# Two memsets of 128x1280 on GpSimd between one field's gathers and the next field's, in a float32 recommendation tower

## The chip, the cores and the metric

One core of a Trainium2 chip. The metric is the time of the whole program on the device in microseconds. Before the change two runs gave 289.72 and 292.36 us, median 291.04.

## The reference

512 samples have 39 fields each. A field's id picks a row of 32 numbers from its table (1000 to 125000 rows). Each pair of fields (i, j) is joined by a 32x32 weight, which gives one number for each of 741 pairs and each sample; these, with 16 dense numbers, go through a small MLP (757 to 512 to 256 to 1).

```python
e = jnp.stack([tbl_0[ids[:, 0]], ..., tbl_38[ids[:, 38]]], axis=1)      # 512 x 39 x 32
z = jnp.einsum('bpc,apc,bpa->bp', e[:, ROW, :], w, e[:, COL, :])        # 741 pairs
h = jnp.concatenate([z, dense_ctx], axis=1)
h = jnp.maximum(h @ W_top1 + b_top1, 0.0)
h = jnp.maximum(h @ W_top2 + b_top2, 0.0)
y = h @ W_top3
```

## The kernel before

The 39 fields are put in an order of 10 blocks of four (the last has three). Blocks 0, 1 and 3 hold twelve fields with tables of 1000 rows, the "hot" ones. Their rows are fetched by one-hot matmuls: SP loads the tables (`tab`) and the ids, ACT and DVE (`rest`, `split`) part each table in three bf16 pieces (`parts`), DVE compares ids with row numbers (L629, into `hot`), and PE multiplies (L688, step `look`): for each hot block eight parts `c`, each of 12 matmuls, which end with one semaphore step of `hot_used`. The last of these look-ups, that of block 3, goes to `z_ps`. Two of the six `rest` steps (L410) are on GpSimd (POOL).

The other seven blocks (2, 4, 5, 6, 7, 8, 9) are gathered. POOL issues for each field four indirect DMAs (L514), each for 128 samples, 27 fields and so 108 gathers in all, into `gathered`, which has three buffers: before block 6 POOL waits until block 2 has been transposed, before block 7 until block 4 has, before block 8 until block 5 has, before block 9 until block 6 has (`turned`). PE transposes a block (L700, step `keep`) when its rows are in; ACT copies it to `eT` (L567) and with DVE makes the split copies in `stack`.

The pairs are then done in 70 groups of tiles (step `tiles`): PE multiplies `stack` with weights from `wring` (L719, 210 matmuls), DVE multiplies the result with `eT` (L658), PE sums over the 32 numbers with `sel` (L735, step `sums`). The ring's chunks are copied by SP from `w_hi` and `w_lo`; the low parts of chunk columns 2 and 3 are made by POOL (L401). Chunk column 2 is first used by group 37, column 3 by group 56. Between the groups lie matmuls of the MLP's first layer (L750, step `early`), whose rounds POOL adds up at the end (L528).

One list, `PLAN`, sets the order of PE, ACT, DVE and SP. In it block 4's transpose stands ahead of group 5, block 5's ahead of group 13, block 6's ahead of group 22, block 7's ahead of group 31, block 8's ahead of group 42, block 9's ahead of group 54. POOL has its own order: gathers block by block, with the four steps of `POOL_WORK` behind the gathers of a field: a `rest` step of hot block 1 (needed for the look-up of block 1) behind block 2's last field, a `rest` step of the third hot block behind block 4's first field, `w_lo` columns 2 and 3 behind block 8's first and last field.

Of the kernel before, what the change touches and what calls it, by code (L numbers as in the profile page):

```python
# [43 lines left out]
P = 128  # L44
# [18 lines left out]
HP = HOT_ROWS // NSLICE  # L63
HOT_BUFS = 4
GATHER_BUFS = 3
STACKS = 3
HOT_FIELDS = [f for f in range(F) if TABLE_ROWS[f] == HOT_ROWS][:G * NHOT]

# [12 lines left out]
def in_block(J):  # L81
    return min(G, F - G * J)
# [140 lines left out]
def turns(J):  # L223

    return TURNS.index(J) + 1
# [48 lines left out]
def dlrm_tower(nc, tables, ids, hot_ids, dense_t, wst, w1, w2, columns, y):  # L274
    with ExitStack() as ctx:
        def sb(name, shape, dt=F32):
            return ctx.enter_context(nc.sbuf_tensor(name, shape, dt))

        def sem(name):
            return ctx.enter_context(nc.semaphore(name))  # L280
# [4 lines left out]
        sel = sb("sel", [P, ZM, K])  # L285
        gathered = sb("gathered", [P, GATHER_BUFS, NCHUNK, P])
        eT = sb("eT", [P, NBLK, B])
        hi_lo = sb("hi_lo", [P, 2, 2, B])
        stack = sb("stack", [P, STACKS, G, B])
        w_lo = sb("w_lo", [P, NWCOL, WCOLS])  # L290
# [7 lines left out]
        b2_sb = columns_sb[:, M1:M1 + M2]  # L298
        w3_sb = columns_sb[:, M1 + M2:]
        y_sb = sb("y_sb", [1, B])  # L300

        room = sb("room", [P, (NZ + M1) * B])
        z_sb = room[:, 0:NZ * B].rearrange("p (k b) -> p k b", k=NZ)
# [60 lines left out]
        stack_lo_made = sem("stack_lo_made")  # L364
        stacked = [sem(f"stacked{i}") for i in range(STACKS)]
        w_hi_made = sem("w_hi_made")
# [15 lines left out]
        y_made = sem("y_made")  # L382
        y_kept = sem("y_kept")
        y_out = sem("y_out")

        mlp_loads = [(w1_sb, w1.rearrange("(k p) n -> p k n", p=P)),
                     (w2_sb, w2.rearrange("(k p) n -> p k n", p=P)),
# [10 lines left out]
        def w_lower(engine, c):  # L398

            engine.wait_ge(w_hi_made, c + 1)  # L400
            engine.tensor_tensor(w_lo[:, c, :].bitcast(F32R), w_lo[:, c, :], w_hi[:, c, :],  # L401
                                 ALU.subtract).then_inc(w_lo_made[c], 1)

        def table_rest(engine, h, i):

            of = slice(G * h, G * h + G)
            engine.wait_ge(part_made, SPLITS.index((h, i)) + 1)
            if i == 1:
                engine.wait_ge(rest_made[h], 1)
            engine.tensor_tensor(parts[2][0:HP, of, :] if i else tab[0:HP, of, :], tab[0:HP, of, :],  # L410
                                 parts[i][0:HP, of, :], ALU.subtract).then_inc(rest_made[h], 1)

        def wait_z(engine, zb):

            engine.wait_ge(z_kept, zb + 1)
            if zb in DENSE_BLOCKS:
                engine.wait_ge(dense_in[zb], 16 * sum(first // P == zb for first, _ in DENSE_ROWS))
# [4 lines left out]
        def _(sp):  # L422
# [35 lines left out]
            for step in PLAN:  # L458
# [3 lines left out]
                if step[0] == "stack":  # L462
                    J = step[1]
                    sp.wait_ge(stack_hi_made, turns(J))
                    sp.wait_ge(stack_lo_made, turns(J))
                    slot = J % STACKS
                    sp.dma_start(stack[P // 2:P, slot, 0:in_block(J), :],
# [23 lines left out]
        @block.gpsimd  # L491
        def _(pool):
            pool.memset(ident[:, :], 0.0).then_inc(consts_zero, 1)
            pool.memset(sel[:, :, :], 1.0).then_inc(consts_zero, 1)
            pool.iota(slice_rows_int[:, :], pattern=[[1, NSLICE]], base=0,
                      channel_multiplier=NSLICE).then_inc(rows_numbered, 1)
            pool.wait_ge(consts_zero, 2)
            pool.affine_select(out=ident[:, :], in_=ident[:, :], compare_op=ALU.not_equal, fill=1.0, base=0,
                               pattern=[[-1, P]], channel_multiplier=1).then_inc(consts_made, 1)

            pool.affine_select(out=sel[:, :, :], in_=sel[:, :, :], compare_op=ALU.is_ge, fill=0.0, base=0,
                               pattern=[[P, ZM], [-K, K]], channel_multiplier=1).then_inc(consts_made, 1)
            pool.wait_ge(consts_made, 2)
            pool.affine_select(out=sel[:, :, :], in_=sel[:, :, :], compare_op=ALU.is_ge, fill=0.0, base=K - 1,
                               pattern=[[-P, ZM], [K, K]], channel_multiplier=-1).then_inc(consts_made, 1)
            pool.wait_ge(ids_in, 16)

            for n, J in enumerate(GATHERED):
                if n >= GATHER_BUFS:
                    pool.wait_ge(turned, n - GATHER_BUFS + 1)  # L510
                for r in range(in_block(J)):
                    f = ORDER[G * J + r]
                    for b in range(NCHUNK):
                        pool.indirect_dma_start(  # L514
                            gathered[:, n % GATHER_BUFS, b, K * r:K * r + K], None, tables[f],
                            bass.IndirectOffsetOnAxis(ap=ids_sb[:, F * b + f:F * b + f + 1], axis=0),
                        ).then_inc(rows_in[J], 16)
                    work = POOL_WORK.get((J, r))
                    if work is not None and work[0] == "rest":
                        table_rest(pool, *work[1:])  # L520
                    elif work is not None:
                        w_lower(pool, work[1])
            for n in range(1, len(ROUNDS)):
                for i, m in enumerate(LAST_FIRST):
                    pool.wait_ge(early_kept, M1 * n + m + 1)
                    if n > 1:
                        pool.wait_ge(early_added, M1 * (n - 2) + i + 1)
                    pool.tensor_tensor(early_sum[0][m], early_sum[0][m], early_sum[n][m],  # L528
                                       ALU.add).then_inc(early_added, 1)

        @block.scalar
        def _(act):
# [3 lines left out]
            for step in PLAN:  # L536
# [31 lines left out]
                elif step[0] == "halve":  # L568
# [4 lines left out]
                    if turns(J) > 2:  # L573
                        act.wait_ge(lo_made, turns(J) - 2)
                    act.activation(hi_lo[0:n, slot, 0, :].bitcast(F32R), eT[0:n, J, :],
                                   ACT.Copy).then_inc(hi_made, 1)
                    if J >= STACKS:
                        act.wait_ge(tiles_made, LAST_GROUP[J - STACKS] + 1)
                    for r in range(in_block(J)):
                        ins = act.activation(stack[0:K, J % STACKS, r, :].bitcast(F32R),  # L580
                                             eT[K * r:K * r + K, J, :], ACT.Copy)
# [32 lines left out]
        def _(dve):  # L614
            for step in PLAN:
                if step[0] == "w_lo":
                    w_lower(dve, step[1])
                elif step[0] == "rest":
                    table_rest(dve, *step[1:])
                elif step[0] == "look":  # L620
                    J, c0, c1 = step[1:]
# [47 lines left out]
        def _(pe):  # L669
# [8 lines left out]
            for step in PLAN:  # L678
# [14 lines left out]
                elif step[0] == "keep" and step[1] in GATHERED:  # L693
                    J = step[1]
                    n = K * in_block(J)
                    at = GATHERED.index(J) % GATHER_BUFS
                    pe.wait_ge(rows_in[J], 16 * in_block(J) * NCHUNK)
# [5 lines left out]
                elif step[0] == "tiles":  # L703
# [10 lines left out]
                    for i, tile in enumerate(tiles):  # L714
                        for k, (src, _) in enumerate(tile):
                            c = passes // WCHUNK
                            if passes % WCHUNK == 0:
                                pe.wait_ge(wring_in[c % WSLOTS], 16 * G * (c // WSLOTS + 1))
                            mm = pe.matmul(t_ps[g % 2][:, i, :],  # L719
                                           wring[:, c % WSLOTS, passes % WCHUNK, :].bitcast(F32R),  # L720
                                           stack[:, J % STACKS, src - G * J, :].bitcast(F32R),
                                           start=(k == 0), stop=(k == len(tile) - 1))
                            passes += 1
# [86 lines left out]
```

## Time and profile before

| | |
|---|---|
| runs, median (lowest to highest) | 291.04 us (289.72 to 292.36) |
| span of the profiled execution | 285.0 us |
| runs' median less that span | 6.0 us |
| PE busy | 198.8 us (70%), 974 matmuls |
| DVE busy | 146.6 us (51%) |
| POOL busy | 134.8 us (47%), of it 104.9 us in 108 gathers |
| ACT busy | 97.5 us (34%) |
| granted TensorE clock, mean | 0.844 |

The span runs from the first to the last instruction of the profiled execution. What the time of a run has beyond it lies before and after the program's instructions; this execution has no time of its own beside the span, so the difference is taken to the median of the two runs. The rows count microseconds from the span's start. The granted clock is 1.00 at 2.4 GHz and 0.50 at 1.2 GHz. "Idle before, releaser" names what ended an engine's wait; "issue" is a wait for nothing that the profile shows, and "remote" is a semaphore whose setter the profile can't name by the time of its record.

### The profile page before, as it was taken

The page shows a single profiled execution, that of the slowest core. Times are in us where ns is not written, and L with a number is a line of the kernel's source. Part 1 is how long each engine was busy: PE and PEld are TensorE (multiplying, and loading weights), DVE is VectorE, ACT ScalarE, POOL GpSimd, SP SyncE. Part 2 cuts the span into 40 slices and gives each one's busy share as a digit, 9 for nine tenths or more (in the row PEclk, how much of TensorE's full clock was granted, in tenths as well). Part 3 has the DMA queues.
Part 4 walks back from the last instruction along what each step waited for, and adds up shares of the span by engine and source line. Part 5 has one row for each costly group of instructions (what it writes and reads, how often), then busy time and mean ns, then how long its engine had stood idle before and what let it go on. Part 6 is the DMA issues. An engine that isn't in the chain of part 4 may idle for free.

```text
span 285.0 us, 2687 instructions
## 1 busy us (share of the span) xinstructions
PE 198.8 (70%) x974; PEld 73.5 (26%) x974; DVE 146.6 (51%) x115; ACT 97.5 (34%) x142; POOL 134.8 (47%) x134
## 2 busy tenths in 40 slices
PE   0048668453212277738798197699899999999996
PEld 0012223000000033213333032243333334344341
DVE  0353794101000027824794266389599779898230
ACT  2516899300000047830540071037127127110032
POOL 7774767777777300776587887200042015007000
PEclk9999797755555559795999669599999999999999
DMA  4869779700000003997266018148715846450000
GB/s 134 257 210 300 285 177 212 164 16 13 14 13 13 9 0 74 300 207 148 50 158 166 12 41 183 41 96 167 167 33 118 183 98 129 98 121 1 0 2 0
DMA packets 11352, 31.40 MB, mean 110 GB/s; under 512 B 3230, under 2 KB 7098, under 8 KB 10379
## 3 DMA queue, kind: packets, MB, share of 16 engines
q1 hardware_dynamic: 7882, 29.45, 42.1%
q0 software_dynamic: 3456, 1.78, 3.5%
q8 instruction: 8, 0.13, 0.2%
q14 instruction: 6, 0.04, 0.0%
HBM read 12.34 MB, written 0.00 MB: 43 GB/s over the span
## 4 chain that ended last, share of the span: by engine, by line
PE 51%; issue 18%; DMA 9%; DVE 7%; SPq 6%; another core or an unknown queue 4%; ACT 3%; DVEq 0%; ACTq 0%
PE t_ps L719 16%; PE z_ps L735 15%; PE z_ps L688 9%; DMA mlp<-tbl 6%; PE side_ps L750 5%; DMA wring<-w_lo 4%; DVE prod L658 3%; SPq L425 2%; PE t_ps L777 2%; DVE prod L629 2%; SPq L431 1%; SPq L475 1%; PE t_ps L765 1%; PE t_ps L770 1%
## 5 line engine op out<-in xcount | busy, mean ns | idle before, releaser
L658 DVE TENSOR_TENSOR prod<-t_ps,eT 128x1536 f32<-128x1536 f32 (+2 forms) x70 | 109.9, 1600 | 79.3 <-PE t_ps L719 49.7
L514 POOL DMA_INDIRECT gathered<-tbl,ids_sb x108 | 104.9, 971 | 53.5 <-issue 31.4
L719 PE MATMUL t_ps<-stack,wring 128*128 128x512 f32 x210 | 72.9, 464 | 12.2 <-issue 6.7
L735 PE MATMUL z_ps<-prod,sel 128*32 128x512 f32 x380 | 57.5, 645 | 4.6 <-issue 4.6
L719 PEld LDWEIGHTS t_ps<-stack,wring 128*128 128x128 f32 x210 | 38.3, 205 | 65.8 <-issue 39.5
L688 PE MATMUL z_ps<-prod,room 125*32 125x512 bf16 x72 | 21.0, 534 | 34.1 <-issue 33.3
L528 POOL TENSOR_TENSOR room<-room,w_hi 128x512 f32<-128x512 f32 x3 | 3.9, 1286 | 66.3 <-ACT w_hi L603 66.3
L629 DVE TENSOR_SCALAR prod<-mlp,slice_rows 125x2048 bf16<-125x2048 f16 x18 | 14.8, 856 | 23.0 <-remote 23.0
L587 ACT ACTIVATE stack<-hi_lo 32x512 fp32r<-32x512 f32 x39 | 24.6, 629 | 2.6 <-issue 1.2
L580 ACT ACTIVATE stack<-eT 32x512 fp32r<-32x512 f32 x39 | 24.4, 625 | 1.0 <-PE t_ps L719 0.7
L750 PE MATMUL side_ps<-room,mlp 128*128 128x512 f32 x32 | 18.4, 660 | 7.7 <-ACT eT L567 7.6
L688 PE MATMUL t_ps<-hot,room 125*32 125x512 bf16 x48 | 6.3, 560 | 18.6 <-DVE hot L629 17.6
L564 ACT ACTIVATE eT<-z_ps 128x512 f32<-128x512 f32 x1 | 0.6, 597 | 50.1 <-PE z_ps L688 50.1
L688 PEld LDWEIGHTS z_ps<-prod,room 125*32 125x32 bf16 x72 | 4.3, 115 | 50.2 <-issue 49.6
L688 PE MATMUL t_ps<-prod,room 125*32 125x512 bf16 x144 | 13.5, 524 | 5.3 <-DVE prod L629 4.8
L735 PEld LDWEIGHTS z_ps<-prod,sel 128*32 128x32 f32 x380 | 8.4, 111 | 30.7 <-issue 24.5
L567 ACT ACTIVATE eT<-side_ps 128x512 f32<-128x512 f32 (+1 forms) x7 | 4.2, 595 | 34.7 <-PE side_ps L700 22.4
L592 ACT ACTIVATE room<-z_ps 128x512 f32<-128x512 f32 x6 | 3.6, 598 | 26.2 <-PE z_ps L735 19.3
L603 ACT ACTIVATE w_lo<-side_ps 128x512 f32<-128x512 f32 x9 | 5.3, 592 | 20.0 <-PE side_ps L750 18.9
L410 DVE TENSOR_TENSOR mlp<-mlp,room 125x1024 f32<-125x1024 f32 x3 | 3.7, 1226 | 15.8 <-issue 13.0
L528 POOL TENSOR_TENSOR room<-room,w_lo 128x512 f32<-128x512 f32 x9 | 11.3, 1286 | 0.0
L554 ACT ACTIVATE room<-mlp 125x1024 bf16<-125x1024 f32 x6 | 6.3, 1054 | 13.7 <-DMA mlp<-tbl 12.4
(49 smaller groups left out, 113.5 us busy)
## 6 DMA issues: line engine op xcount, KB each, us to landing
wring<-w_hi SPq DMA_DIRECT2D x30, 224.0 KB
wring<-w_lo SPq DMA_DIRECT2D x30, 224.0 KB
stack<-stack SPq DMA_DIRECT2D x9, 512.0 KB
w_lo<-wst SPq DMA_DIRECT2D x4, 896.0 KB, 15.2
eT<-hot_ids SPq DMA_DIRECT2D x3, 1024.0 KB
gathered<-tbl,ids_sb POOLq DMA_INDIRECT x108
mlp<-w SPq DMA_DIRECT2D x1, 1536.0 KB
mlp<-tbl SPq DMA_DIRECT2D x12, 125.0 KB
```

Of the source, the lines that this page charges most:

```text
L425: sp.dma_start(tab[0:HP, n, :], tables[HOT_FIELDS[n]].rearrange("(p c) d -> p (c d)", c=NSLICE))\
L514: pool.indirect_dma_start(gathered[:, n % GATHER_BUFS, b, K * r:K * r + K], None, tables[f], bass.IndirectOffsetOnAxis(ap=ids_sb[:, F * b ...
L528: pool.tensor_tensor(early_sum[0][m], early_sum[0][m], early_sum[n][m], ALU.add).then_inc(early_added, 1)
L554: act.activation(parts[i][0:HP, of, :], tab[0:HP, of, :], ACT.Copy).then_inc(part_made, 1)
L580: ins = act.activation(stack[0:K, J % STACKS, r, :].bitcast(F32R), eT[K * r:K * r + K, J, :], ACT.Copy)
L587: ins = act.activation(stack[K:2 * K, J % STACKS, r, :].bitcast(F32R), hi_lo[K * r:K * r + K, turns(J) % 2, 1, :], ACT.Copy)
L629: dve.tensor_scalar(hot[n % HOT_BUFS][0:HP, :, :], ids_half[J % 2][0:HP, :, :], slice_rows[0:HP, c:c + 1], None, ALU.is_equal).then_inc(ho ...
L658: dve.tensor_tensor(prod[:, g % XSLOTS, 0:n, :], t_ps[g % 2][:, 0:n, :], field, ALU.mult).then_inc(multiplied, 1)
L688: mm = pe.matmul(look_ps[J][K * r:K * r + K, :], parts[i][0:HP, G * J + r, K * c:K * c + K], hot[n % HOT_BUFS][0:HP, r, :], start=(c == 0 ...
L719: mm = pe.matmul(t_ps[g % 2][:, i, :], wring[:, c % WSLOTS, passes % WCHUNK, :].bitcast(F32R), stack[:, J % STACKS, src - G * J, :].bitcas ...
L735: mm = pe.matmul(z_ps[K * (u % G):K * (u % G) + K, :], sel[:, u // G, :], prod[:, g % XSLOTS, t - TILE_BASE[g], :], start=(u < G), stop=(u ...
L750: mm = pe.matmul(side_ps[:, :], w, x, start=(i == 0), stop=last)
```

## The change

A new scratch tile `pause` of 128x1280 float32. Behind the four gathers of every field, and ahead of the `POOL_WORK` step that may follow them, POOL clears it twice. Each of these memsets waits on the semaphore `paused` until all earlier ones are complete. Nothing reads the tile.

```diff
+PAUSE = 1280
+PAUSES = 2
@@
+        pause = sb("pause", [P, PAUSE])
@@
+        paused = sem("paused")
+        pauses = []
@@
+        def rest_a_while(engine):
+
+            for _ in range(PAUSES):
+                if pauses:
+                    engine.wait_ge(paused, len(pauses))
+                engine.memset(pause[:, :], 0.0).then_inc(paused, 1)
+                pauses.append(None)
@@
                             bass.IndirectOffsetOnAxis(ap=ids_sb[:, F * b + f:F * b + f + 1], axis=0),
                         ).then_inc(rows_in[J], 16)
+                    rest_a_while(pool)
                     work = POOL_WORK.get((J, r))
```

On POOL, from the first gather on, the kernel before has this order (L514 gathers, 128x32 each; L410 the two `rest` steps):

```order
L514 DMA gathered<-tbl,ids_sb 128x32 x16
L410 TENSOR_TENSOR room<-mlp,room 125x1024
L514 DMA gathered<-tbl,ids_sb 128x32 x4
L410 TENSOR_TENSOR room<-mlp,room 125x1024
L514 DMA gathered<-tbl,ids_sb 128x32 x64
```

The changed kernel has at the same place:

```order
L527 DMA gathered<-tbl,ids_sb 128x32 x4
L423 MEMSET pause 128x1280 x2
L527 DMA gathered<-tbl,ids_sb 128x32 x4
L423 MEMSET pause 128x1280 x2
L415 TENSOR_TENSOR room<-mlp,room 125x1024
L527 DMA gathered<-tbl,ids_sb 128x32 x4
L423 MEMSET pause 128x1280 x2
L415 TENSOR_TENSOR room<-mlp,room 125x1024
L527 DMA gathered<-tbl,ids_sb 128x32 x4
L423 MEMSET pause 128x1280 x2
```

Two memsets now stand behind each four gathers, so that the first `rest` step has four pairs ahead of it and the second has five. The other place is block 8 and 9, the last gathers. Before:

```order
L401 TENSOR_TENSOR w_lo<-w_lo,w_hi 128x1792
L514 DMA gathered<-tbl,ids_sb 128x32 x12
L401 TENSOR_TENSOR w_lo<-w_lo,w_hi 128x1792
L514 DMA gathered<-tbl,ids_sb 128x32 x12
```

And changed, from the first of these `w_lo` steps on:

```order
L406 TENSOR_TENSOR w_lo<-w_lo,w_hi 128x1792
L527 DMA gathered<-tbl,ids_sb 128x32 x4
L423 MEMSET pause 128x1280 x2
L527 DMA gathered<-tbl,ids_sb 128x32 x4
L423 MEMSET pause 128x1280 x2
L527 DMA gathered<-tbl,ids_sb 128x32 x4
L423 MEMSET pause 128x1280 x2
L406 TENSOR_TENSOR w_lo<-w_lo,w_hi 128x1792
L527 DMA gathered<-tbl,ids_sb 128x32 x4
L423 MEMSET pause 128x1280 x2
```

Here too a pair follows every field, three of them between the two `w_lo` steps. The other engines' orders are as before.

## Rows read from the trace of the kernel before

**Rows 1.** The page: span, PE's busy tenths in 40 slices, a load's time to landing.

```profile
span 285.0 us, 2687 instructions
...
PE   0048668453212277738798197699899999999996
...
ids_sb<-ids SPq DMA_DIRECT2D x1, 78.0 KB, 1.9
```

**Rows 2.** Busy by stretch: PE, PEld, DVE, ACT, POOL; granted clock, DMA share, GB/s.

```profile
40.30:47.10 6.80, 5.79 (x76) 2.31 (x77) 5.11 (x8) 6.65 (x12) 5.24 (x6) 0.75 0.98 203
52.00:77.00 25.00, 10.98 (x24) 1.74 (x24) 1.59 (x2) 1.09 (x2) 18.92 (x20) 0.52 0.20 40
77.00:96.00 19.00, 4.10 (x7) 0.71 (x7) 0.00 (x0) 0.00 (x0) 14.37 (x16) 0.50 0.07 13
96.00:103.00 7.00, 2.83 (x5) 0.40 (x4) 0.00 (x0) 0.00 (x0) 0.00 (x0) 0.50 0.01 2
...
212.00:236.00 24.00, 23.71 (x118) 8.66 (x116) 20.49 (x14) 9.03 (x15) 5.67 (x5) 1.00 0.64 137
236.00:285.00 49.00, 46.75 (x200) 18.42 (x196) 30.02 (x23) 12.85 (x21) 7.88 (x7) 1.00 0.22 47
```

**Rows 3.** Timeline of the look-ups: start, duration, engine, line, idle before and releaser.

```profile
32.49 1.47 PE L688 MATMUL t_ps<-hot,room 125*32 125x512 bf16 x12 [2.69 <-DVE hot L629]
...
66.83 0.83 DVE L629 TENSOR_SCALAR prod<-mlp,slice_rows 125x2048 bf16<-125x2048 f16 x1 [10.48 <-remote]
...
80.12 0.59 PE L688 MATMUL z_ps<-prod,room 125*32 125x512 bf16 x1 [2.21 <-issue]
...
103.20 0.60 ACT L564 ACTIVATE eT<-z_ps 128x512 f32<-128x512 f32 x1 [50.10 <-PE z_ps L688]
```

**Rows 4.** Timeline, three more waits for results of PE.

```profile
25.60 2.08 DVE L629 TENSOR_SCALAR prod<-mlp,slice_rows 125x2048 bf16<-125x2048 f16 x3 [3.65 <-remote]
...
162.44 0.60 ACT L567 ACTIVATE eT<-side_ps 128x512 f32<-128x512 f32 x1 [12.35 <-remote]
...
179.89 0.60 ACT L592 ACTIVATE room<-z_ps 128x512 f32<-128x512 f32 x1 [6.89 <-remote]
```

**Rows 5.** Groups of POOL by line: count, busy us, mean ns, idle before.

```profile
L514 POOL DMA_INDIRECT gathered<-tbl,ids_sb x108 | 104.9, 971 | 53.5 <-issue 31.4 <-PE side_ps L700 21.7 <-DMA ids_sb<-ids 0.4
...
L410 POOL TENSOR_TENSOR room<-mlp,room 125x1024 bf16<-125x1024 f32 x2 | 4.9, 2434 | 6.5 <-ACT room L554 6.5
...
L504 POOL TENSOR_SCALAR_AFFINE_SELECT sel<-sel 128x256 f32<-128x256 f32 x1 | 0.4, 445 | 0.1
L494 POOL MEMSET sel<- 128x256 f32 x1 | 0.3, 312 | 0.0
...
L493 POOL MEMSET ident<- 128x128 f32 x1 | 0.2, 205 | 0.3 <-POOLq L802 0.3
```

**Rows 6.** Timeline of POOL, where bursts of gathers begin or have ended.

```profile
27.22 2.44 POOL L410 TENSOR_TENSOR room<-mlp,room 125x1024 bf16<-125x1024 f32 x1 [3.88 <-ACT room L554]
...
37.76 2.42 POOL L410 TENSOR_TENSOR room<-mlp,room 125x1024 bf16<-125x1024 f32 x1 [2.67 <-ACT room L554]
...
113.61 1.25 POOL L514 DMA_INDIRECT gathered<-tbl,ids_sb  x1 [17.68 <-PE side_ps L700]
...
137.76 0.94 POOL L514 DMA_INDIRECT gathered<-tbl,ids_sb  x1 [3.99 <-PE side_ps L700]
...
142.46 4.06 POOL L401 TENSOR_TENSOR w_lo<-w_lo,w_hi 128x1792 fp32r<-128x1792 f32 x1
...
161.38 3.98 POOL L401 TENSOR_TENSOR w_lo<-w_lo,w_hi 128x1792 fp32r<-128x1792 f32 x1
...
179.54 0.94 POOL L514 DMA_INDIRECT gathered<-tbl,ids_sb  x1 [0.30 <-issue]
```

**Rows 7.** Line 700, transposes of block 7 and of block 9: first and last start.

```profile
L700 PE MATMUL side_ps<-ident,gathered x4: 270/272/272, 188.4 to 188.7; 128*128 128x128 f32 x4
...
L700 PE MATMUL side_ps<-ident,gathered x4: 273/273/315, 236.0 to 236.3; 128*96 128x128 f32 x4
```

## The prediction

> **What bounds the kernel now.** I read the page first. TensorE (PE) shows tenths 3, 2, 1, 2, 2 in the five slices from 64 to 100 us, and 8 or 9 from 185 us to the end [rows 1]. So there are two kernels in one: a late part that TensorE bounds, and an early part in which nearly nothing runs. The table by stretch says the same: from 212 to 236 us PE is busy 23.7 of 24.0 us, from 236 to 285 us 46.8 of 49.0, both at full clock; but from 52 to 77 us it runs 24 matmuls, from 77 to 96 us 7, and DVE, ACT and the DMA engines stand idle too. Only GpSimd (POOL) works there, 14.4 of 19.0 us: it issues gathers [rows 2].
>
> Next I asked the timeline who waits. PE in that stretch is in the last one-hot look-up (L688, hot block 3, 96 matmuls). Each matmul's record is 0.6 us, but they start 2.8 us apart "by issue", while the same line ran 76 matmuls in 6.8 us from 40.3 us [rows 2, 3]. DVE waits 10.48 us and ACT 50.10 us for its results [rows 3]. Three more places have the same sign, a "remote" wait for a PE result whose matmuls had long been recorded: 3.65 us to 25.60, 12.35 us to 162.44, 6.89 us to 179.89 [rows 4].
>
> The last view is POOL's timeline. Gathers run in bursts: 3.0 to 23.3, 29.8 to 35.1, 40.3 to 95.9, 113.6 to 133.8, 137.8 to 142.4, 146.7 to 161.4, 165.5 to 180.5 (108 gathers; where POOL did or awaited something else stands in [rows 6], with the wait that tells when the burst before it ended). All four late releases stand inside or just behind a burst of 12 or more gathers: 25.60 is 2.3 us after one ended, 162.44 is 1.1 us after, 179.89 within the last gather. The long stretch ends at 103, 7.1 us after the last of 44 gathers in a row. After 180.5 us there are no gathers and no such wait. And the two bursts of only four gathers passed without harm. So my reading is that PE's work completes late while gathers are issued without a break, that the lag grows with the length of the burst (slow from some 5 us into it), and that it drains in 1 to 7 us after it. In the stretch from 45 to 103 us 7 of that look-up's 8 parts of 12 matmuls complete; at the rate of [rows 2], 6.8 us for 76 matmuls, these 84 take 7.5 us. Some 50 us are lost there.
>
> **The change, part by part.** Behind every fourth gather come two memsets of 128x1280, each waiting for the one before: 27 times, 54 memsets, also before the two `rest` and the two `w_lo` steps that POOL carries.
>
> One memset: the trace has none of that size. Two others give a line, 205 ns for 128 columns and 312 ns for 256 [rows 5]: 0.84 ns a column, so 0.31 + 1024 x 0.84 ns = 1.17 us. From below, the slope without a fixed part gives 1.07 us. From above, 312/256 = 1.22 ns a column gives 1.56 us; the two-input subtraction, 2434 ns for 1024 columns [rows 5], would give 3.0 us, but it reads two tensors and this reads none. I take 1.17, since a slope of two memsets is the nearest thing.
>
> One pause: 2 x 1.17, plus 0.1 for the wait between them (as before L504, [rows 5]), less 0.14 because a gather follows other work after 0.16 us and a gather after 0.30 (31.4 us over 105 [rows 5]): 2.3 us. Four gathers take 4 x 1.25 = 5.0 us, so a field takes 7.3 us.
>
> POOL's last gather starts at 179.5 now [rows 6]. Ahead of it are 26 pauses, 59.8 us. But POOL also waits today: 21.7 us for transposes and 6.5 us for ACT [rows 5]. A POOL that is late for those finds them done: 179.5 + 59.8 - 28.2 = 211.1 us. Nothing shows how long a gather takes to land; the id load's 1.9 us [rows 1] is the nearest row, so block 9 is there at 213.0. Counting back by 7.3 us a field and 4.1 us for each `w_lo` step: block 8 at 187.0, block 7 at 153.7, block 6 at 124.5, block 5 at 95.3, block 4 at 66.1.
>
> PE's side. The first hot look-up loses or wins little. The `rest` step of hot block 1 goes from 27.2 to 32.5 (four pauses, 9.2 us, less the 3.88 us that it waits today [rows 6]); it ends at 35.0, and PE starts that look-up 2.5 us later than today's 32.5 [rows 3]. The last look-up then starts near 45.5. With pauses it should run as it did from 40.3 to 47.1, and be done near 56 instead of 103; up to 65 if some lag stays. The stretch after it (loads of the MLP, the ring) took from 103 to 137.6, when block 5 is turned [rows 6]; shifted, block 5 is turned at 91 to 100. From then on the gathers are late, not PE. Blocks 6 and 7 are 9 tile groups apart, 7 and 8 are 11 and 8 and 9 are 12; a group takes 2.1 us today (23 groups from 188.4 to 236.0, [rows 7]). So after block 6 at 124.5 PE reaches block 7's transpose at 143.4 and waits to 153.7; reaches block 8's at 177 and waits to 187.0; reaches block 9's at 211.5 and waits to 213.0. POOL's `w_lo` chunk 2 is done near 165 and is first used 6 groups behind block 7, 166: a ring load may cost 3 us there, inside the 10 us of wait that follow.
>
> From block 9's transpose to the end it is 285.0 - 236.0 = 49.0 us of full PE, with no gather in it today or then. 213.0 + 49.0 = 262.0. One more us for a lower clock behind the waits (the granted clock was 0.50, 1.2 GHz, where PE had stood nearly idle, [rows 2]): 263. Outside the span the runs have 291.04 - 285.0 = 6.0 us more; so 269.
>
> Note how robust that is: the end hangs on 52 memsets and 49.0 us, and the last look-up may end anywhere up to about 90 us without moving it.
>
> **A rule against this.** The trace shows PE's results late only with long gather bursts [rows 3, 4, 6]. The Trainium skill, page "SBUF — State Buffer", section "Who interferes with whom", says that "PE and ACT never wait on anyone" and that only VectorE and GpSimd share ports. By that rule the slow stretch has another cause, pauses can't shorten it, and the time is that of the second rival, 294 us, where the rows give 269.
>
> **Rivals.**
> *Some lag stays, or the memset is dearer.* With 1.56 us a memset 52 of them add 20 us: 289. If each burst of four still holds PE back 2 to 3 us, a block costs PE some 32 us, more than the 29.2 of its gathers, and the end moves by some 10 us: 279.
>
> *The slow stretch is not the gathers' doing.* For it: PE stays slow for 7 us after 95.9 us, with POOL at rest (0.00 busy, [rows 2]). Then the look-up ends where it does, plus 2.5 us. Blocks 4 to 9 land at 66, 95, 125, 154, 187, 213, before they are turned today (113.5, 137.6, 154 to 162, 188.4, 211, 236.0 [rows 4, 6, 7]), so the 60 us on POOL are hidden: 287.5 + 6 = 294, no change that can be measured. The Trainium skill's "SBUF — State Buffer" speaks for this one.
>
> *Slower: pauses too short.* The lag of the longest burst took 7.1 us to drain, a pause is 2.4. If 2.4 us drains nothing, the last look-up stays starved until POOL stops by itself, at the wait for block 4's transpose, after block 6's last gather. Ahead of that gather are 15 pauses, 34.5 us, less the 6.5 us of waits that go: it moves by 28 us, and everything behind it moves along: 285 + 28 + 6 = 319. It decides where the look-up ends after 90 us. Against it: after the short bursts nothing had to drain at all.
>
> **Chances.** A measurement of this kernel tells 2% from no change. Forecast 0.60 (257 to 276). Lag or dearer memset 0.18 (276 to 291), of which 0.14 is faster by over 2% and 0.04 within it. Gathers not the cause 0.10 (292 to 296), within 2%. Starved to 122.6 us 0.12 (from 297 on). Faster 0.74, same 0.14, slower 0.12. The range 257 to 291 holds the first two and the edge of the third; the lower end is the 1.07 us memset (5 us less) and an earlier landing.
>
> **What would show it.** Right: the memset's mean near 1170 ns; the last L688 matmul before 70 us; POOL's last gather near 211 us with no wait for transposes; PE waiting for gathers ahead of blocks 7, 8 and 9; 49 us from block 9's transpose to the end. Wrong: matmuls of L688 still 1 to 3 us apart up to 100 us or beyond; "remote" waits of 5 us and more with pauses in place; a memset far from 1.2 us; or PE idle for something other than gathers between 70 and 210 us, such as the ring behind `w_lo`.

## The result, and the profile after

The changed kernel takes 270.24 us (two runs, 269.99 and 270.49) against 291.04: ratio 0.929, with a 95% interval of 0.919 to 0.940. Faster, as forecast, and 1.2 us from the predicted 269. Ratios compare only the runs within 1.5% of their kernel's fastest (of the 13 runs of before in the first experiments these are two), while each time given is the median of all runs, so the two need not agree to the last per cent. The page of the changed kernel, with the tenths of PE and POOL in 40 slices of 6.7 us, the granted clock, and the chain that ended last:

```profile
span 268.8 us, 2741 instructions
...
PE   0048047766059609960698239909989979999996
...
POOL 7888899888988888888888888888988899115000
PEclk9999859799858965996599957977999999999999
...
POOL 66%; PE 16%; issue 12%; DMA 4%; DVE 1%; ACT 0%; POOLq 0%; DVEq 0%
POOL gathered L527 39%; POOL pause L423 22%; PE z_ps L749 4%; PE t_ps L733 4%; POOL w_lo L406 3%; DMA gathered<-tbl,ids_sb 3%; PE t_ps L791 3%; POOL room L415 2%; PE t_ps L779 1%; PE t_ps L784 1%; PE side_ps L764 1%; DVE prod L672 1%; PE side_ps L714 1%; DMA ids_sb<-ids 1%; PE z_ps L797 1%
```

The row of 3, 2, 1, 2, 2 of [rows 1] is gone, and the chain runs through GpSimd: gathers and pauses are 61% of it. From 67 us on PE's zeros are waits of up to 11.4 us for gathered rows, but for the one near 177 us, which is told below. The timeline at the end of the last look-up, the counterpart of [rows 3], and at the last gather (start, duration, engine, line, idle before and releaser):

```profile
57.55 0.83 PE L702 MATMUL z_ps<-prod,room 125*32 125x512 bf16 x12 [0.82 <-DVE prod L643]
58.49 0.60 ACT L578 ACTIVATE eT<-z_ps 128x512 f32<-128x512 f32 x1 [2.01 <-PE z_ps L702]
...
216.01 0.94 POOL L527 DMA_INDIRECT gathered<-tbl,ids_sb  x1 [0.30 <-issue]
...
219.24 0.64 PE L714 MATMUL side_ps<-ident,gathered 128*96 128x128 f32 x4 [1.51 <-DMA gathered<-tbl,ids_sb]
```

ACT has block 3 at 58.5 us, not at 103.2. The last gather starts at 216.0, not at 179.5 [rows 6]; 3.2 us later PE transposes block 9, having waited for its rows, and from there to the end it is 49.6 us. POOL's groups, with the wait of PE for gathered rows from the list of waits:

```profile
L527 POOL DMA_INDIRECT gathered<-tbl,ids_sb x108 | 108.4, 1004 | 29.0 <-issue 28.1 <-PE side_ps L714 0.3 <-DMA ids_sb<-ids 0.3
L423 POOL MEMSET pause<- 128x1280 f32 x54 | 64.8, 1200 | 1.6
```

```profile
PE side_ps L714 <- DMA gathered<-tbl,ids_sb: 40.2, 5, 11.4
```

The 21.7 us for which POOL waited for transposes [rows 5] are 0.3 us now; instead PE waits 40.2 us for gathers. The bound has changed sides.

One stop of PE has another cause. Ahead of group 37, the first to use chunk column 2, it stood still for 6.7 us (PE's timeline; the second line is from the list of SP's waits: total, times, longest):

```profile
180.91 1.62 PE L733 MATMUL t_ps<-stack,wring 128*128 128x512 f32 x3 [6.69 <-issue]
...
SPq L454 <- POOL w_lo L406: 25.0, 1, 25.0
```

SP had to wait for POOL's first `w_lo` step, which ended at 171.5 us, before it could issue the copies of that column into the ring, from 171.5 us on; from 174.2 to 181.0 us the DMA engines were 99% busy. The profile names no releaser, so that PE waited for the ring is read from this order. It costs nothing here, since block 8's rows came at 192.2 us only.

### The profile page after: what moved, and what is told of

The parts are those of the page before. It is cut to its first block, busy times and chain, and to the rows that moved or that the text cites. A ratio compares the mean times of both kernels' runs of the same rounds, so it can differ in the third digit from the quotient of the medians.

```text
span 268.8 us, 2741 instructions
## 1 busy us (share of the span) xinstructions
PE 179.9 (67%) x974; PEld 71.7 (27%) x974; DVE 155.0 (58%) x115; ACT 97.5 (36%) x142; POOL 203.5 (76%) x188
## 4 chain that ended last, share of the span: by engine, by line
POOL 66%; PE 16%; issue 12%; DMA 4%; DVE 1%; ACT 0%; POOLq 0%; DVEq 0%
POOL gathered L527 39%; POOL pause L423 22%; PE z_ps L749 4%; PE t_ps L733 4%; POOL w_lo L406 3%; DMA gathered<-tbl,ids_sb 3%; PE t_ps L791 3%; POOL room L415 2%; PE t_ps L779 1%; PE t_ps L784 1%; PE side_ps L764 1%; DVE prod L672 1%; PE side_ps L714 1%; DMA ids_sb<-ids 1%; PE z_ps L797 1%
## 5 line engine op out<-in xcount | busy, mean ns | idle before, releaser
L527 POOL DMA_INDIRECT gathered<-tbl,ids_sb x108 | 108.4, 1004 | 29.0 <-issue 28.1
L733 PE MATMUL t_ps<-stack,wring 128*128 128x512 f32 x210 | 71.4, 456 | 12.5 <-issue 7.7
L423 POOL MEMSET pause<- 128x1280 f32 x54 | 64.8, 1200 | 1.6
L749 PE MATMUL z_ps<-prod,sel 128*32 128x512 f32 x380 | 56.5, 632 | 0.0
L714 PE MATMUL side_ps<-ident,gathered 128*128 128x128 f32 (+1 forms) x28 | 6.4, 370 | 40.4 <-DMA gathered<-tbl,ids_sb 40.2
L702 PE MATMUL t_ps<-hot,room 125*32 125x512 bf16 x48 | 5.0, 542 | 25.3 <-DVE hot L643 15.1
L643 DVE TENSOR_SCALAR prod<-mlp,slice_rows 125x2048 bf16<-125x2048 f16 x18 | 18.3, 1051 | 2.0 <-PE z_ps L702 1.8
L714 PEld LDWEIGHTS side_ps<-ident,gathered 128*128 128x128 f32 (+1 forms) x28 | 4.1, 182 | 44.5 <-DMA gathered<-tbl,ids_sb 43.9
L702 PE MATMUL t_ps<-prod,room 125*32 125x512 bf16 x144 | 12.4, 497 | 5.1 <-DVE prod L643 5.1
L657 DVE TENSOR_TENSOR hi_lo<-eT,hi_lo 128x512 fp32r<-128x512 f32 (+1 forms) x10 | 9.2, 917 | 4.2 <-ACT eT L581 2.0
```

What stands on the lines that cost most here:

```text
L423: engine.memset(pause[:, :], 0.0).then_inc(paused, 1)
L527: pool.indirect_dma_start(gathered[:, n % GATHER_BUFS, b, K * r:K * r + K], None, tables[f], bass.IndirectOffsetOnAxis(ap=ids_sb[:, F * b ...
L643: dve.tensor_scalar(hot[n % HOT_BUFS][0:HP, :, :], ids_half[J % 2][0:HP, :, :], slice_rows[0:HP, c:c + 1], None, ALU.is_equal).then_inc(ho ...
L702: mm = pe.matmul(look_ps[J][K * r:K * r + K, :], parts[i][0:HP, G * J + r, K * c:K * c + K], hot[n % HOT_BUFS][0:HP, r, :], start=(c == 0 ...
L714: mm = pe.transpose(side_ps[0:n, P * b:P * b + P], gathered[:, at, b, 0:n], ident[:, :])
L733: mm = pe.matmul(t_ps[g % 2][:, i, :], wring[:, c % WSLOTS, passes % WCHUNK, :].bitcast(F32R), stack[:, J % STACKS, src - G * J, :].bitcas ...
```

## Experiments: does the length of a burst of gathers matter?

The theory: on a long row of gathers PE's results come late; a pause lets them drain; with pauses the end hangs on GpSimd's queue. The first four kernels ran on one chip (the result files name it 14; they name none for the result above), where the kernel before took 293.3 us (13 runs, 286.3 to 295.1).

**One memset.** `PAUSES = 1`.

> One memset behind each field in place of two. Theory (bursts of gathers hold TensorE's results back, a pause lets them drain; the end of the changed kernel hangs on GpSimd's queue): 26 x 1.25 us fewer ahead of the last gather, so it starts near 184 us instead of 216, the last look-up still ends before 65 us, and the time is 238 to 248 us. Rival (a pause of 1.2 us drains too little): look-up ends at 90 us or later, time 275 us or more. Rival (the memsets' length is what counts, not GpSimd's queue): as the change, 270.

242.9 us, ratio 0.832 (0.825 to 0.840), as expected. POOL's rows:

```profile
L527 POOL DMA_INDIRECT gathered<-tbl,ids_sb x108 | 105.2, 974 | 29.4 <-issue 28.6 <-DMA ids_sb<-ids 0.4
L423 POOL MEMSET pause<- 128x1280 f32 x27 | 32.0, 1185 | 0.0
...
181.50 0.94 POOL L527 DMA_INDIRECT gathered<-tbl,ids_sb  x1 [0.30 <-issue]
```

The look-up ends at 54.3 us, the last gather starts at 181.5. A pause of 1.2 us is nearly enough there: two waits for late results are left, of 1.2 us at the look-up's end and of 4.5 us at 103 us. The other half of the change's pauses costs 27 us, by 270.2 us in the result above; the changed kernel itself was not run on chip 14 beside this one. This version beats the kernel before by 50 us on this chip.

**A hold in place of pauses.** No memset; the row of gathers begins once the look-ups are done.

```diff
+                    if (J, r) == (4, 1):
+                        pool.wait_ge(hot_used, NHOT * NSLICE)
                     for b in range(NCHUNK):
```

> No memsets at all; GpSimd waits, behind the first field of block 4, until all look-ups are done (hot_used at 24), then gathers without pause. Theory: the last look-up runs at full rate and ends near 56 us, but then 60 gathers follow one another and hold back the tile groups instead: block 5's transpose comes not much before 130 us, GpSimd having stopped at its wait for it, and the time is 270 to 290 us. Rival (only the look-ups suffer, for a reason of their own): 240 to 250 us. Rival of the skill's rule that TensorE waits for nobody: the look-up stays slow, ends at 100 us, time 291.

291.8 us against 293.3, ratio 1.013 (1.006 to 1.022): nothing won, and 2 us over the top of what I had expected. The look-up was fast (ACT has block 3 at 52.6 us), and the tile groups behind it were starved instead. Timeline of DVE, with PE's matmuls for the last of the three, and the busy table of two stretches (length, then busy us and count of PE, PEld, DVE, ACT, POOL; granted clock, DMA share, GB/s):

```profile
89.90 1.23 DVE L660 TENSOR_TENSOR prod<-t_ps,eT 128x1024 f32<-128x1024 f32 x1 [12.79 <-remote]
101.10 1.22 DVE L660 TENSOR_TENSOR prod<-t_ps,eT 128x1024 f32<-128x1024 f32 x1 [9.97 <-remote]
102.38 1.65 PE L721 MATMUL t_ps<-stack,wring 128*128 128x512 f32 x3 [7.62 <-issue]
131.19 1.76 DVE L660 TENSOR_TENSOR prod<-t_ps,eT 128x1536 f32<-128x1536 f32 x1 [28.87 <-remote]
```

```profile
104.00:143.00 39.00, 8.83 (x29) 3.54 (x29) 6.94 (x4) 0.00 (x0) 17.34 (x19) 0.50 0.17 32
143.00:170.00 27.00, 22.61 (x112) 8.71 (x110) 17.85 (x13) 12.74 (x21) 21.81 (x18) 0.94 0.46 98
```

Here 60 gathers follow one another from 50.8 to 126.8 us. The three matmuls recorded from 102.4 to 104.0 us are handed to DVE at 131.2, 4.4 us after the last of them. So it isn't the look-up's bf16 matmuls, nor its place in the program: the float32 matmuls of the tile groups are delivered late too beside a long row of gathers. It also shows that a fast look-up is worth nothing here if the row of gathers only moves (the hold itself keeps POOL for 10.0 us).

**Only the late pauses.** The memsets behind fields of blocks 7, 8 and 9.

```diff
-                    rest_a_while(pool)
+                    if J >= 7:
+                        rest_a_while(pool)
```

> Two memsets behind each field of blocks 7, 8 and 9 only; blocks 2 to 6 are gathered as before the change. Theory: the look-up is slow as before and ends at 103 us; block 4's transpose at 113; the two later stalls (150 to 163 and 175 to 181 us, some 15 us) go; GpSimd's last gather starts near 200 us; time 272 to 282 us. Rival (the later waits are not the gathers' doing): 291 us.

270.1 us, ratio 0.924 (0.915 to 0.933); I had expected 272 to 282. The look-up is as slow as before:

```profile
104.20 0.60 ACT L579 ACTIVATE eT<-z_ps 128x512 f32<-128x512 f32 x1 [50.59 <-remote]
```

```profile
77.00:96.00 19.00, 4.24 (x8) 0.72 (x7) 0.00 (x0) 0.00 (x0) 14.43 (x16) 0.50 0.10 13
...
115.00:195.00 80.00, 68.66 (x342) 28.09 (x341) 60.76 (x42) 34.43 (x53) 68.88 (x62) 0.94 0.69 152
```

But from 115 to 195 us PE is busy 68.7 of 80 us beside gathers with pauses (before: 58.8 of 80), and block 9 is transposed at 218.6, 17 us earlier than in [rows 7]. The late stalls were worth some 20 us, more than the 15 I had read from [rows 4]. It takes as long as the changed kernel, but by another bound: here the last gather starts at 199.7 us and PE is the one that is late, there PE waits for the last gather.

**The same 54 memsets, in lumps.** Eight behind each block.

```diff
-                    rest_a_while(pool)
+                    if r == in_block(J) - 1:
+                        for _ in range(in_block(J)):
+                            rest_a_while(pool)
```

> The same 54 memsets, but eight together behind each block (six behind the last) instead of two behind each field, so that bursts are of 12 to 16 gathers. Theory (length of a burst counts): TensorE gets its results late from some 5 us into each burst, the last look-up ends at 62 to 70 us, each block costs some 33 us or more instead of 29, and the time is 275 to 295 us. Rival (it is enough that the gathers are spread over more time, or that the memsets are there): GpSimd's queue is 4 memsets shorter ahead of the last gather, so 265 us.

281.2 us, ratio 0.963 (0.954 to 0.972), within the 275 to 295 of the theory, though its last gather starts at 214.3, before that of the changed kernel. PE gets to block 9's transpose at 230.0, not at 219.2. The list of waits has the late results again, which the changed kernel's has not:

```profile
DVE prod L674 <- remote: 45.2, 7, 9.7
```

The same work on GpSimd, the same spread over time, other burst lengths: 11 us more than the changed kernel's 270.2, which it got in another set of runs. The length of the burst counts.

## Experiments: the pause, and another chip

The next four ran together, and the kernel before took 222.6 us there (7 runs, 220.9 to 223.4), 70 us less than on chip 14. This was chip 12.

**A half memset and two short ones.** `PAUSES = 1, PAUSE = 640`, and `PAUSES = 2, PAUSE = 128`.

> One memset of 128x640 behind each field, a pause of some 0.65 us. Theory (a lag builds from some 5 us into a burst and needs a pause to drain): GpSimd's queue is 14 us shorter than with one memset of 128x1280, which no longer bounds alone, but part of the lag stays; look-up ended by 65 us, time 232 to 252 us. If a pause of 0.65 us drains nothing: 270 us or more.

> Two memsets of 128x128 behind each field, 0.5 us together. Theory (it is the length of the pause that counts): most of the lag is back, look-up ends between 65 and 95 us, time 255 to 285 us. Rival (any break in the row of gathers is enough, since another kind of instruction comes between): 230 to 240 us.

231.5 us, ratio 1.041 (1.034 to 1.048), and 228.7 us, ratio 1.027 (1.020 to 1.033). As times they lie just under ranges that I had given (from 232 us and from 230 us); but the ratios say that on this chip each pause only costs, since there was nothing to drain: neither trace has a "remote" wait of DVE or ACT. The kernel before left no trace on chip 12; that its long rows of gathers do no harm there is read from its time. Neither expectation had a place for that.

**Waits for landing.** Behind each field GpSimd waits for its four gathers.

```diff
+                    pool.wait_ge(rows_in[J], 16 * NCHUNK * (r + 1))
                     work = POOL_WORK.get((J, r))
```

> No memset: behind each field GpSimd waits until its four gathers have landed. Theory (the pause counts, not the memset): look-up ends by 65 us, no waits of TensorE's results over 5 us; a wait of 1 to 2.3 us a field gives 238 to 270 us. Rival (the memsets themselves help, or gathers in flight do no harm and the instructions between them matter): look-up slow as before, 285 us or more.

277.8 us, ratio 1.250 (1.241 to 1.258), 8 us over the 238 to 270 that I had expected. POOL waits 68.5 us for landings, so its last gather starts at 222.8 us and PE waits for rows:

```profile
L514 POOL DMA_INDIRECT gathered<-tbl,ids_sb x108 | 106.4, 986 | 94.1 <-DMA gathered<-tbl,ids_sb 68.5 <-issue 24.8 <-DMA ids_sb<-ids 0.3
```

A wait until the rows have landed, 68.5 us in 22 waits, so 3.1 us each, costs more than two memsets. On this chip it could not tell whether the pause or the memset helps.

**Plain copies.** The gathers replaced, so that the ids pick nothing.

```diff
-                        pool.indirect_dma_start(
-                            gathered[...], None, tables[f], bass.IndirectOffsetOnAxis(...))
+                        pool.dma_start(gathered[...], tables[f][P * b:P * b + P, :])
```

> The kernel before with each of the 108 gathers replaced by a plain copy of 128 table rows from GpSimd's queue, so that the ids don't pick the rows and the output is another. If any transfer that GpSimd makes descriptors for holds TensorE back, the look-up is slow (ends near 100 us if the copies take as long as gathers to issue, 0.94 us). If only the gather with indices does, the look-up runs at full rate and ends near 56 us, and the time is 220 to 245 us.

217.2 us, ratio 0.974 (0.966 to 0.983), 3 us under the range for a fast look-up. A copy holds GpSimd for 0.55 us, a gather for 0.97. As before was fast there too, nothing follows about the cause.

The next three went to chip 10, where before took 291.7 us (7 runs, 286.8 to 294.2).

**Both kernels again.** No edit.

> The kernel before, unchanged, for a trace on the chip of this call: in one call its runs took 286 to 295 us, in another, on another chip, 221 to 223. Theory now (gathers in a row hold TensorE back on some chips or at some times only): either 286 to 295 us with the slow look-up and the late results, or 219 to 225 us with the last look-up ended before 60 us, no waits for TensorE's results over 5 us, and 44 gathers in a row all the same. A time between these would speak for an effect that varies by degrees.

> The changed kernel, unchanged. Its end hangs on GpSimd's queue (216 us to the last gather, 3 to land, 49.6 to the end), which no lag enters: 267 to 271 us whichever chip it is. So 0.92 of before where gathers hold TensorE back, and 1.20 to 1.22 of before where they don't. Rival (the chip where before took 222 us is faster in all): some 205 to 215 us.

Before: 289.1 us (283.6 to 292.6). After: 270.3 us (269.2 to 271.1), ratio 0.939 (0.929 to 0.949). The lag is there, but takes another shape: in this execution of the kernel before the last look-up's matmuls are recorded by 60.1 us, ACT has their result at 78.3, and the tile groups pay more:

```profile
57.63 2.45 PE L688 MATMUL z_ps<-prod,room 125*32 125x512 bf16 x15 [0.73 <-issue]
...
78.30 0.60 ACT L564 ACTIVATE eT<-z_ps 128x512 f32<-128x512 f32 x1 [23.26 <-remote]
...
DVE prod L658 <- remote: 36.3, 8, 9.4
```

The four runs of the kernel before spread over 9 us. The changed kernel's four spread over 2, as they should if its end hangs on GpSimd's queue.

**Short pauses again.** The same file as on chip 12.

> Two memsets of 128x128 behind each field, on the chip of this call. Where gathers hold TensorE back: 255 to 285 us if a pause of 0.5 us drains little, 228 to 235 if any break is enough. Where they don't: 227 to 231 us as it was, a few us over before.

282.9 us in the middle, from 273.4 to 287.8, against 228.7 on chip 12. One program, two chips, the same stretch of 51 to 103 us; chip 12 first, then chip 10 (an execution of 287.8 us):

```profile
51.00:103.00 52.00, 36.86 (x176) 15.10 (x172) 35.86 (x26) 26.61 (x39) 41.55 (x56) 0.89 0.74 175
```

```profile
51.00:103.00 52.00, 17.95 (x44) 4.50 (x40) 1.50 (x2) 2.04 (x4) 39.42 (x58) 0.51 0.18 33
...
104.75 0.60 ACT L578 ACTIVATE eT<-z_ps 128x512 f32<-128x512 f32 x1 [51.68 <-remote]
```

POOL is as busy with gathers and memsets in both, 41.6 and 39.4 us; PE gives 176 matmuls on the one and 44 on the other. On chip 10 a break of 0.5 us is not enough, where 1.2 us nearly was on chip 14.

**Plain copies again.**

> The kernel before with plain copies of 128 table rows in place of the gathers (the ids pick nothing, the output is another), now hoped for on a chip where before takes 286 to 295 us. There: if any transfer from GpSimd's queue holds TensorE back, the look-up ends at 75 us or later and the time is 240 us or more; if only the gathers with indices do, 215 to 222 us as on the other chip. Where before takes 222 us: 215 to 222 us, which tells nothing new.

It fell on chip 12 once more (before 223.1 us): 217.8 us, ratio 0.977 (0.972 to 0.982). Of the copies it tells nothing new. But the runs on chip 10 lie between the two sets on chip 12, which gave 222.6 and 223.1 us; that speaks for a difference between the chips rather than between moments.

## Why the prediction was right, point by point

*The reading of the slow stretch.* Right on the chips where it could be tested. Pauses took it away, the longest waits for PE's results moved with the long rows of gathers wherever these were put (hold, late pauses, lumps), and a fast look-up with the row merely moved brought nothing. That the gathers are what delays PE is shown by the length of the burst; by which path they do it is not. One sentence of the reading was wrong: there is such a wait after 180.5 us, 2.5 us behind the last burst, where it fits the theory as well as the others:

```profile
182.96 2.98 DVE L658 TENSOR_TENSOR prod<-t_ps,eT 128x1024 f32<-128x1024 f32 x2 [7.40 <-remote]
```

Nor are there four late releases but ten; the other five are DVE's at 49.2, 55.6, 137.0, 158.1 and 163.8, all inside a burst of 12 or more or within 3.3 us of its end.

*The memset.* 1.20 us measured, 1.17 taken. The line through two small memsets held at five times the size; it was 0.03 x 52 = 1.6 us short. A pair mostly took 2.41 us, so the wait between two costs hardly anything, where the working had 0.1 us.

*POOL's queue.* The last gather was to start at 211.1 and started at 216.0. Some 3.5 us of these 4.9 are the gathers, which held GpSimd for 108.4 us and not 104.9: four took 1.6 to 2.3 us. The pauses were about 1 us dearer than the 59.8 of the working. The waits of 28.2 us did go.

*Landing.* 1.9 us taken from a plain load, 3.2 us from the last gather's start to PE's transpose. Short by 1.3 us.

*PE's side.* The last look-up ended at 58.4 us (56 forecast). I had thought that blocks 4 and 5 would be there in time; block 4's rows came at 76.7, and PE waited 8.8 us for them and 9.1 us for block 5's, which cost nothing, since the end doesn't hang there. For block 7 it waited 9.4 us, as forecast (10). For block 8 another 10 us were forecast and only the weight load waited, 0.6 us: the time had gone into the 6.7 us in which PE stood behind the ring and `w_lo`, for which the working allowed 3. That was on my list of signs of being wrong, and it came true without moving the end, which hangs on POOL.

*The tail.* 49.6 us, with 49.0 and 1 taken.

*Span and time.* Here the working had its largest wrong terms, and they cancelled. I added 6.0 us for what lies outside the span: the runs' median less the profiled span. In the runs here that have both, 270.49 us stands beside a span of 268.8, 283.63 beside 281.9: it is 1.7 us. By that the profiled execution of the kernel before took some 286.7 us, one of the shorter ones of a kernel whose runs spread over 9 us. So the span was 5.8 us too low (263 for 268.8: 4.9 from POOL's queue, 1.3 from the landing, less 0.4 from the tail) and the part outside it 4.3 us too high, and it is luck that 269 comes so close; with 1.7 in place of 6.0 the same working gives 264.7.

*The rivals.* "The slow stretch is not the gathers' doing" fell on chips 14 and 10. The Trainium skill, page "SBUF — State Buffer", section "Who interferes with whom", has it that TensorE never waits on anyone. It says so of SBUF's ports, and no trace here tells whether the delay comes by a port. What fell is what I had drawn from it, that gathers can't hold PE back: no run on chip 12 speaks against that, the traces on chips 14 and 10 do (44 matmuls on chip 10 for 176, above). "Pauses too short" fell for 1.2 and 2.4 us; with 0.5 us on chip 10 the look-up did stay slow, at 273 to 288 us. "Some lag stays" was not seen in the changed kernel, and once, as 4.5 us, with one memset. None of my cases was the one that matters most: that some chips don't show the lag at all, and that the forecast's sign would hang on that.

*What the change is worth without the lag.* It was not run on chip 12. From what was: the kernel there that waits for landings has its last gather at 222.8 and ends at 277.8 us; the changed kernel's last gather starts at 216.0, and its queue holds only 0.3 us of waiting for PE. So I would expect some 270 us, 1.21 times the 222.6 of before. That is argued, not shown.

*Open.* What differs between the chips; whether any transfer from GpSimd's queue does the harm or only a gather with indices; the shortest pause that is enough between 0.5 and 1.2 us; and what one memset costs on chip 12 (half a memset cost 4%). The runs fell on a chip by chance, and those two that could have told the second fell both on chip 12. The waits for landing fell there too, so that no run tells a memset from a mere wait as the cure. And each run on record has a span and a granted clock, so each was recorded as it ran; whether the lag is there without recording is not shown.

## What to carry to other kernels

When an engine is slow with nothing to wait for, look at what the idle-looking engine beside it does without a break, and move that; a pause on an engine off the critical path was worth 21 us here, and 50 us at half its length. So make the pause as short as it works: from two memsets to one gave 27 us more, because the pauses had become the bound. And time the kernel before again on another chip before a fix like this is kept: here one memset gives 0.83 on one chip, and shorter pauses cost 3 to 4% on another, where there is nothing to cure.

## What the runs showed that I had not expected

The kernel before takes 221 to 226 us on one chip and 284 to 295 on two others, with the same 108 gathers; within one chip its spread is 2 to 4%.

DVE was held up too, in another way. In the kernel with one memset, behind block 9's transpose (DVE, then POOL):

```profile
189.58 4.46 DVE L657 TENSOR_TENSOR hi_lo<-eT,hi_lo 96x512 fp32r<-96x512 f32 x1
...
189.77 3.73 POOL L542 TENSOR_TENSOR room<-room,w_lo 128x512 f32<-128x512 f32 x3
```

A subtraction of two SBUF operands that takes 0.69 us elsewhere takes 4.46 us and ends 0.5 us after POOL's three additions end; another, at 138.6 us beside POOL's `w_lo` step, takes 4.99. The tail of that kernel is 54.2 us (186.4 to 240.6) for 49.6. The Trainium skill, "SBUF — State Buffer", "Who interferes with whom", says that such an instruction contends with a GpSimd instruction that reads SBUF; this trace agrees. The memsets did DVE less harm, but not none. In the changed kernel a comparison and the first memset of a pair start together:

```profile
23.90 2.84 POOL L423 MEMSET pause<- 128x1280 f32 x2
23.95 1.68 DVE L643 TENSOR_SCALAR prod<-mlp,slice_rows 125x2048 bf16<-125x2048 f16 x1 [0.21 <-PE t_ps L702]
```

The comparison takes 1.68 us and not 0.73, the pair 2.84 and not 2.41. In the kernel with one memset POOL's round of additions, early now because its gathers end early, has become the next thing to move.
